# Two adjacent stages of a post-norm transformer kernel joined into one block, with the second stage's weight built inside the first

## The reference, cut to what matters

```
# sub-layer 5: 4-layer convolution stack on a 64-wide state (depth scan)
h = x @ Win.T + bin                                   # 512 -> 64
for i in range(4):
    y = silu(layernorm(h));  h = h + sconv(y) * sc    # a linear recurrence over the tokens
    y = silu(layernorm(h) @ W1.T + b1) @ W2.T + b2    # 64 -> 256 -> 64
    h = h + y
f5 = layernorm(h) @ Wout.T + bout                     # 64 -> 512
# sub-layer 6: dense layer with bias and two low-rank adapters (rank 64, scale 1/4)
f6 = x @ W_base.T + b_base + 0.25 * ((x @ A.T + x @ WL.T) @ B.T + (...) @ WR.T)
```

## Time and profile before

| quantity | value |
|---|---|
| median of three runs | 1443.9 us |
| time of the profiled execution | 1441.58 us |
| its span, first to last instruction | 1439.8 us |
| mean granted TensorE clock | 0.940 |
| busy: TensorE matmul / VectorE / ScalarE / GpSimd | 1294.9 / 745.1 / 431.1 / 151.4 us |
| start of the convolution block (first load issued) | 631.27 us |
| last instruction of the two-adapter block ends | 854.55 us |

### The profile page before, as it was taken

One profiled execution on the slowest core, in us unless ns is written; L12 is line 12 of the kernel. 1 busy time (PEld: TensorE's weight loads), 2 busy tenths in 40 slices (PEclk: granted clock), 3 DMA queues, 4 the chain that ended last, 5 costly groups with the idle time before them and its releaser, 6 DMA issues. The chain is left out here.

```text
span 1439.8 us, 14790 instructions
## 1 busy us (share of the span) xinstructions
PE 1294.9 (90%) x5410; PEld 853.0 (59%) x5410; DVE 745.1 (52%) x1297; ACT 431.1 (30%) x717; POOL 151.4 (11%) x208
## 2 busy tenths in 40 slices
PE   7999998799799999983887788989999998799998
PEld 4787665344578787772665343444454443488876
DVE  5222323484676645414576555877777632433264
ACT  2222211120311214200322112146666666221141
POOL 0000000000294000001111022001011114000000
PEclk9999999799899999975998799989999999899999
DMA  7110000730355530022000010000000000112000
GB/s 313 45 44 0 0 0 7 322 146 1 131 198 197 197 109 0 1 73 87 0 0 0 0 44 1 0 1 2 1 2 3 2 3 1 45 66 81 7 23 37
DMA packets 18072, 78.83 MB, mean 55 GB/s; under 512 B 2946, under 2 KB 3586, under 8 KB 15843
## 3 DMA queue, kind: packets, MB, share of 16 engines
q1 hardware_dynamic: 18018, 78.13, 14.8%
HBM read 75.76 MB, written 2.10 MB: 54 GB/s over the span
## 5 line engine op out<-in xcount | busy, mean ns | idle before, releaser
L373 PE MATMUL psum<-L_ffn_x,L_ffn_w_up 128*128 128x512 f32 x1152 | 264.3, 391 | 3.1 <-DVE L_ffn_hidden L502 3.1
L373 PEld LDWEIGHTS psum<-L_ffn_x,L_ffn_w_up 128*128 128x128 f32 x1152 | 217.0, 189 | 50.2 <-DVE L_ffn_hidden L502 5.0
L1830 DVE TENSOR_REDUCE mqa_top<-psum 128x1 f32<-128x512 f32 (+3 forms) x304 | 186.1, 657 | 57.4 <-PE psum L1656 37.7
L1749 ACT ACTIVATE mqa_prob<-psum 128x512 f32<-128x512 f32 x288 | 159.8, 601 | 85.7 <-PE psum L1674 84.5
L390 PE MATMUL psum<-L_ffn_wd,L_ffn_part_h 128*128 128x512 f32 x600 | 142.7, 399 | 7.0 <-DVE L_ffn_wd L298 7.0
L1674 PE MATMUL psum<-mqa_stack,mqa_keys 100*128 100x512 f32 x288 | 132.8, 476 | 4.8 <-DMA mqa_stack<-mqa_rows 3.5
L390 PEld LDWEIGHTS psum<-L_ffn_wd,L_ffn_part_h 128*128 128x128 f32 x600 | 114.9, 193 | 32.0 <-DVE L_ffn_part_h L289 7.8
L1645 PE MATMUL psum<-mqa_keys,mqa_stack 96*128 96x512 f32 (+1 forms) x256 | 107.3, 438 | 2.3 <-DVE mqa_top L1830 1.0
L373 PE MATMUL psum<-L_attn_x,L_attn_w_up 128*128 128x512 f32 x456 | 105.4, 393 | 3.9 <-DVE L_attn_hidden L502 3.9
L373 PEld LDWEIGHTS psum<-L_attn_x,L_attn_w_up 128*128 128x128 f32 x456 | 86.6, 190 | 22.5 <-issue 4.3
L1674 PEld LDWEIGHTS psum<-mqa_stack,mqa_keys 100*128 100x128 f32 x288 | 55.3, 196 | 72.1 <-ACT mqa_prob L1749 62.6
(11 more groups left out here) (247 smaller groups left out, 1716.3 us busy)
## 6 DMA issues: line engine op xcount, KB each, us to landing
L_ffn_stage<-in_L_w SPq DMA_DIRECT2D x25, 768.0 KB, 6.3
L_ffn_z_int<-in_L_z SPq DMA_DIRECT2D x14, 768.0 KB, 4.3
L_ffn_s_all<-in_L_s SPq DMA_DIRECT2D x14, 768.0 KB, 6.1
lora_wo<-in_L_wo SPq DMA_DIRECT2D x8, 1024.0 KB, 8.6
L_attn_stage<-in_L_w SPq DMA_DIRECT2D x10, 512.0 KB, 3.6
L_attn_w_down<-in_L_down SPq DMA_DIRECT2D x1, 2560.0 KB, 24.3
x_feat<-in_x_feat SPq DMA_DIRECT2D x2, 1024.0 KB, 7.2
x_tok<-in_x_tok SPq DMA_DIRECT2D x1, 2048.0 KB, 18.8
```

The costliest lines, as they stand in the source:

```text
L373: ins = nc.tensor.matmul(bank[half][:, :], w_up[:, slot, w_part, at:at + P], x[:, x_part, k, half * HALF:(half + 1) * HALF], start=k == 0 ...
L1749: nc.scalar.activation(prob[:, n % PROBS, :], score_bank[n % 3], ACT.Exp, scale=SCALE)\
L1830: nc.vector.tensor_reduce(top[:, i % 2, lo // HALF, heads[0]:heads[-1] + 1], max_bank[n % 3][:, 0:len(heads) * width] .rearrange("p (h k) ...
```

## The change: what it does, and the diff

The two blocks become one. `two_loras` is gone, and `conv_stack` receives its weights object, which now also owns `w_eff`, the sums and their semaphores.

1. SyncE waits for `loaded` (three loads) before it issues the ten loads of `load_ahead`.
2. GpSimd adds the adapter halves and scales one sum, before its first `root`; it no longer copies `W1` and the column constants.
3. The loops over the four layers are unrolled; layers read `w1_all[:, i]` and `cols[:, i]` directly.
4. Each layer i makes column block i of `W_eff` on TensorE: one matmul from the sums and one with the identity that adds the base weight; ScalarE copies the result out. The filler at a layer's end is 5 matmuls long, not 9. Eight filler matmuls stand ahead of the input projection and eight behind it.
5. The tail of sub-layer 5 and the product and tail of sub-layer 6 run as one pipeline: at step t come tile t of the first, and tile t-2 of the second. The second tail has banks 0 to 3 and semaphores of its own.
6. The bias is added to `x_tok` by GpSimd, after the tile's transposes and before the second tail's addition; VectorE's own bias addition (L97) is gone.

```diff
@@ sync
                 sp.dma_start(high[:, :], a["C_high"]).then_inc(loaded, 16)
+                sp.wait_ge(loaded, LOADS)
                 load_ahead(sp)
@@ gpsimd
-                def prepare(i, first):
-                    if not first:
-                        pool.wait_ge(ff_ready, 4 * i)
-                    nc.gpsimd.tensor_copy(w1[:, :], w1_all[:, i, :]).then_inc(w1_ready, 1)
-                    if not first:
-                        pool.wait_ge(hidden_ready, 4 * i)
-                    nc.gpsimd.tensor_copy(col[:, :], cols[:, i, :]).then_inc(col_ready, 1)
-                    root(2 * i)
-                    root(2 * i + 1)
-                prepare(0, True)
-                with pool.Fori(1, C_DEPTH) as i:
-                    prepare(i, False)
+                pool.wait_ge(two.loaded, 32)
+                nc.gpsimd.tensor_tensor(two.low_sum[:, :], two.low[:, 0, :], two.low[:, 1, :], ALU.add)\
+                    .then_inc(two.summed, 1)
+                nc.gpsimd.tensor_tensor(two.high_sum[:, :], two.high[:, 0, :], two.high[:, 1, :], ALU.add)\
+                    .then_inc(two.summed, 1)
+                pool.wait_ge(two.summed, 2)
+                nc.gpsimd.tensor_scalar(two.high_sum[:, :], two.high_sum[:, :], two.SCALING, None, ALU.mult)\
+                    .then_inc(two.summed, 1)
+                for n in range(2 * C_DEPTH):
+                    root(n)
                 root(2 * C_DEPTH)
+                pool.wait_ge(two.base_loaded, 32)
+                for t in range(NT):
+                    pool.wait_ge(tail.transposed, tail.base + t + 1)
+                    nc.gpsimd.tensor_tensor(c.x_tok[:, t, :], c.x_tok[:, t, :], two.bias[:, :], ALU.add)\
+                        .then_inc(two.biased, 1)
@@ tensor
+                keep_busy(8)
                 pe.wait_ge(in_loaded, 16)
...
-                    keep_busy(9)
+                    pe.wait_ge(two.summed, 3)
+                    pe.wait_ge(two.base_loaded, 32)
+                    nc.tensor.matmul(ff_bank[3][:, :], two.low_sum[:, i * P:(i + 1) * P], two.high_sum[:, :],
+                                     start=True, stop=False)
+                    nc.tensor.matmul(ff_bank[3][:, :], c.ident[:, :], two.base[:, i, :], start=False, stop=True)\
+                        .then_inc(two.made, 1)
+                    keep_busy(5)
+                keep_busy(8)
                 pe.wait_ge(const, 7)
-                with pe.Fori(0, C_DEPTH) as i:
+                for i in range(C_DEPTH):
                     layer(i)
...
+                pe.wait_ge(two.eff_ready, KC)
+                for t in range(NT + 3):
+                    if t < NT:
+                        if t >= 2:
+                            pe.wait_ge(tail.out_taken, tail.base + t - 1)
+                        nc.tensor.matmul(tail.out_bank[t % 2][:, :], normed2[:, t * P:(t + 1) * P], w_out[:, :],
+                                         start=True, stop=True).then_inc(tail.out_ready, 1)
+                    if 1 <= t <= NT:
+                        tail.pe(pe, t - 1)
+                    if 2 <= t < NT + 2:
+                        pe.wait_ge(tail.feat_ready, tail.base + t - 1)
+                        product_tiles(c, pe, tail_two, two.w_eff, t - 2)
+                    if t >= 3:
+                        tail_two.pe(pe, t - 3)
@@ scalar
+                    act.wait_ge(two.made, i + 1)
+                    nc.scalar.copy(two.w_eff[:, i, :], ff_bank[3][:, :]).then_inc(two.eff_ready, 1)
...
+                for t in range(NT + 3):
+                    if t < NT:
+                        tail.act_std(act, t)
+                    if 1 <= t <= NT:
+                        tail.act_copy(act, t - 1)
+                    if 2 <= t < NT + 2:
+                        tail_two.act_std(act, t - 2)
+                    if t >= 3:
+                        tail_two.act_copy(act, t - 3)
@@ vector
-                for t in range(NT):
-                    tail.dve(dve, t)
+                for t in range(NT + 2):
+                    if t < NT:
+                        tail.dve(dve, t)
+                    if t >= 2:
+                        dve.wait_ge(two.biased, t - 1)
+                        tail_two.dve(dve, t - 2)
```

More of the change, by code:

```diff
@@ L70, with __init__ @@
     NAMES = ("out_ready", "out_taken", "ln_step", "var_ready", "std_ready", "normed", "transposed", "feat_ready")
-    def __init__(self, chip, out_bank, tr_bank, last=False):
+    def __init__(self, chip, out_bank, tr_bank, last=False, sems=None):
         self.c, self.out_bank, self.tr_bank, self.last = chip, out_bank, tr_bank, last
         (self.out_ready, self.out_taken, self.ln_step, self.var_ready, self.std_ready, self.normed,
-         self.transposed, self.feat_ready) = chip.tail_sems
-        self.base = NT * chip.tails
-        chip.tails += 1
+         self.transposed, self.feat_ready) = chip.tail_sems if sems is None else sems
+        if sems is None:
+            self.base, self.steps = NT * chip.tails, chip.ln_steps
+            chip.tails += 1
+        else:
+            self.base, self.steps = 0, [0]
     def dve(self, dve, t, bias=None):
@@ L1164, in _ @@
                 ins.then_inc(h_in, 1)
-                def keep_busy(times):
-                    for _ in range(times):
-                        nc.tensor.matmul(ff_bank[0][:, 0:256], c.ident[:, :], rot.wave[:, 0, 0:256],
-                                         start=True, stop=True)
                 def transposes(n):
@@ L1195, in layer @@
                     transposes(2 * i + 1)
-                    pe.wait_ge(w1_ready, i + 1)
                     for half in range(2):
                         pe.wait_ge(n2_ready, 2 * i + half + 1)
+                        if i and half == 1:
+                            pe.wait_ge(two.eff_ready, i)
                         for f in range(FT):
-                            nc.tensor.matmul(ff_bank[2 * half + f][:, :], w1[:, f * P:(f + 1) * P],
+                            nc.tensor.matmul(ff_bank[2 * half + f][:, :], w1_all[:, i, f * P:(f + 1) * P],
                                              normed2[:, half * HALF:(half + 1) * HALF],
@@ L1236, in affine @@
                                              ACT.Identity, scale=weight, bias=bias).then_inc(n2_ready, 1)
-                with act.Fori(0, C_DEPTH) as i:
-                    act.wait_ge(col_ready, i + 1)
+                for i in range(C_DEPTH):
                     for half in range(2):
@@ L1305, in _ @@
                 PRE, STEPS = state_of["count"], 30
-                with dve.Fori(0, C_DEPTH) as i:
+                for i in range(C_DEPTH):
                     state_of["count"], state_of["base"] = PRE, STEPS * i
```

47 lines of the change are left out of this document (23 added, 24 removed).

## The result

The changed kernel takes 1424.99 us (median of 4 runs, 1422.25 to 1426.36); the kernel before, run beside it, 1443.57 (4 runs, 1441.13 to 1444.46). The ratio is 0.9876, 95% interval 0.9858 to 0.9893: faster by 18.6 us. The forecast was 1419.5 us, with a range of 1412 to 1429. The profiled executions took 1441.58 and 1424.28 us, 17.3 apart, where the sum of the prediction said 23.2.

A forecast was written before the change was run, and what follows sets the result against it. Bound by no engine in the layers, by VectorE then TensorE in turn behind them, by `conv_high` at the start. 22.2 + 0.8 + 1.2 - 1.0 = 23.2 us gave 1418.4, 1420.7 against the median; forecast 1419.5, range 1412 to 1429.

The forecast's parts named there:

- the sum of the prediction: All terms together against the profiled execution: 23.2 us gained, 1441.6 to 1418.4 us.
- Joined tails: Tails of sub-layers 5 and 6 in one loop: VectorE sets a 5.30 us period, 22.2 us gained.
- Bias on GpSimd: Joined loop: the 1.27 us addition per tile is hidden; 1 us charged for disturbing VectorE, bounds 0 and 10.
- rival 1: Joined loop: GpSimd and VectorE block each other in every tile, 10 us less gain, 1429.5 us; chance 0.09.
- SyncE's wait: Start of the block: holding back ten loads brings `conv_high` 4.0 us earlier, bounds 0 and 5.
- rival 2: Start: the ten loads are what delays `conv_high`, so `loaded` comes early; 11 us gained there, 1410 us; chance 0.07.
- The first root: GpSimd's first root at the start: 6.9 us after `loaded`, not 3.3; start's net gain 1.2 us, bounds -4 and 4.
- The halves: Start: adapter halves `two_low` and `two_high`, issued only after `loaded`, land 3.5 us after it.
- The scaling: GpSimd's scaling of an adapter sum before the first root: 0.8 us taken, from 0.4 to 1.3.
- Filler ahead of the projection: Start, TensorE: at most 7.4 us of filler at half clock, projection ends near 653, before the load; nothing gained or lost.
- Layers: Four unrolled convolution layers: 0.2 us saved in each, 0.8 us gain, bounds 0 and 2; making the adapter weight there costs nothing.
- Two of its signs: Signs of being right: attention's first matmul 23 us earlier; `loaded` 26 to 28 us after `conv_high` is issued.

The follow-up runs named there:

- Experiment 8: Changed kernel with the two tails one after the other, adapter weight still made in the layers, bias still on GpSimd: 1431.38 us, ratio 0.9913.
- experiment 1: Changed kernel with GpSimd's adapter additions and scaling moved from ahead of the first root to behind the second: 1419.28 us, ratio 0.9847.
- experiment 4: Changed kernel without SyncE's wait for `loaded`, its ten loads issued at once again: 1426.68 us, ratio 0.9899.
- experiment 3: Changed kernel with the 97-partition load `conv_high` issued as two, 96 partitions and 1: 1405.73 us, ratio 0.9753.
- Experiment 2: Changed kernel with a one-column dummy Silu on ScalarE ahead of its wait for the loads, so its table loads early: 1423.53 us, ratio 0.9874.
- the repeat: The changed kernel measured once more, with no edit: 1423.03 us, ratio 0.9864.
- experiments 9 and 10: Changed kernel with split load, later sums, early table; filler behind folding 7 to 4 matmuls, or behind first transposes 4 to 7: 1404.07 and 1404.90 us.
- experiment 5: The kernel before with only the 97-partition load issued as 96 and 1: 1428.19 us, ratio 0.9903.

## Why the prediction was right, and where it was not

*Joined tails, 22.2 forecast, 22.04 measured: right*, by its own steps. Period 5.30 us, clock at the upper level, the first product's four matmuls (eight records) 4.82 us for 4.3 (partly at the lower level), the end 52.06 us behind the first out matmul, where the sum had 51.9. (Its last addition, 827.6 + 2.75 + 1.7, makes 832.05 and not 832.3, and the copy's 1.51 and 0.58 us make more than 1.7; both slips are small.) Experiment 8 adds what the prediction didn't part: 13.0 of it needs no overlap.

*Bias on GpSimd, 1.0 charged of bounds 0 to 10: right*, and rival 1 false. The two pass each other, by as little as 0.04 us; only two of VectorE's steps were clearly longer. That the lock was real and the price small is shown by experiment 1's 1.48 us for 0.42.

*SyncE's wait, 4.0 us forecast, 4.8 measured, 5.0 by experiment 4: right in size.* By the load's own issue it was 6.1 us, above the bound of 5, so the ten loads had cost it more than "a few us"; the later issue took 1.3 back. The load's one engine was read rightly too, from the share of 0.06; rival 2 needed "loaded" within 12 us and is false. But the prediction used this finding only to bound the change. What it was worth, experiment 3 shows: 19 us.

*The first root is the step that failed.* The start was to gain 1.2 us and lost 2.05 to the first `y`. Three terms were mis-sized or missing:

- The halves: 3.5 us from "loaded" to their landing were taken from an issue of 0.5 us and 2.5 us for 256 KB. Measured 5.6: the two landed 3.9 and 4.5 us after their issues.
- The scaling: taken as 0.8 between two rows, measured 1.49, above the dearer bound of 1.3. Here 64x512 times a constant takes GpSimd longer than the addition of two such tensors (1.25). The root came 9.61 and not 6.9 us after "loaded".
- The table load, 1.28 us, was in no term. Experiment 2 shows it on the path. That ScalarE meets this load only behind its wait for the transposes was not read from the code.

Against that, two roots run back to back once the first can (2.02 us for both), since both variances were waiting.

*Filler ahead of the projection, nothing forecast: true of the sum, wrong in its reason.* The projection was to run at half clock and end near 653. It ran at the upper level and ended at 644.8, behind filler of 6.32 us; that bought nothing only because the load came at 658.96.

*Layers, 0.8 us gain forecast, 0.44 lost, 0.25 gained in the repeat: no gain shown.* The period where the clock holds is 26.42 us for 26.86, a gain of 0.44 each, twice what was forecast. (The prediction's 3.86 us for the two new matmuls and five of filler is 4.0 by its own prices, which changes nothing.) But the filler behind the folding is slow where the clock falls, and VectorE waits for what is queued behind it. Two layers of the changed kernel, filler and the row addition that waits, each:

```profile
734.72 5.41 PE L1116 MATMUL psum<-wave,ident 128*128 128x256 f32 x14
...
746.91 0.42 DVE L1305 TENSOR_TENSOR conv_h<-conv_h,psum 128x256 f32<-128x256 f32 x1 [7.23 <-PE psum L1164]
...
761.64 3.24 PE L1116 MATMUL psum<-wave,ident 128*128 128x256 f32 x14
...
773.33 0.42 DVE L1305 TENSOR_TENSOR conv_h<-conv_h,psum 128x256 f32<-128x256 f32 x1 [5.92 <-PE psum L1164]
```

Filler of 5.41 us, idle of 7.23 us; filler of 3.24, idle of 5.92. The granted clock is 0.59 over the first and 1.00 over the second. These seven matmuls (fourteen records) took 3.24 to 5.87 us over all kernels that have them, slow in different layers. What sets in which layer the clock falls stays open; experiments 9 and 10 moved it and did not explain it.

*After the block, nothing forecast, 1.04 us lost* to the first `mqa_k_full`, and 0.35 between the last copy and attention's first matmul. The first was 6.08 to 6.69 us in every kernel with the joined loop, and 5.46 in experiment 8, which has all of the change but that loop. So it belongs to the joined loop. The two stretches, of the kernel before and of the changed one:

```profile
855.02:860.54 5.52, 5.51 (x9) 2.44 (x10) 1.79 (x4) 0.00 (x0) 5.14 (x9) 0.68 0.44 147
```

```profile
835.89:842.45 6.56, 6.56 (x9) 2.87 (x10) 1.79 (x4) 0.00 (x1) 6.09 (x10) 0.57 0.52 166
```

TensorE is busy all through both, at a clock of 0.68 and 0.57. In the kernel before the clock is at the lower level from 851.7 to 858.5 us, 3.5 us of it in attention's matmuls; in the changed kernel from 834.7 to 841.5, 5.6 us of it. So the 1.04 us are the clock's, which fell later against attention's first matmul, 1.2 us ahead of it for 3.3. In the kernel before it fell in TensorE's pause ahead of the last transposes (849.7 to 852.8 us), in the changed one just behind them (they end at 834.4). What sets the moment isn't shown. The 0.35 us don't belong to the loop: that gap was 0.46 to 0.48 or 0.82 to 0.83 us in kernels with it, and 0.82 in experiment 8.

*The whole.* Of the 5.8 us between the sum (23.2) and the spans (17.4) the start has 3.25, the layers 1.24, attention's beginning 1.04 + 0.35, the 580 us behind it 0.7 and the time ahead of the block 0.07; the joined stage with the bias gave 0.84 more than the sum had. The direction and the main mechanism stand; the start's terms were mis-sized. The forecast of 1419.5 lay 1.2 us below the 1420.7 that the sum gives, and no term stands for that. Two of its signs were missed: attention's first matmul came 19.1 us earlier and not 23, and "loaded" 25.0 us after the load's issue and not 26 to 28.

## What to carry to other kernels

When the share of the DMA engines is one sixteenth during the wait that ends last, look at that load's partition count before anything else is tuned: here splitting 97 into 96 and 1 was worth as much as the whole restructuring. Work moved onto an idle engine is only free if it is put behind the small step for which the others wait; price what its inputs need to land too, from the moment they are issued. When two blocks are joined, part the gain into what is no longer waited for and what overlaps, since the first can often be had alone.

## What the runs showed that was not expected

- A load of 97 partitions and 596 kB is in 25 us after its issue and moves 26 GB/s; as 96 and 1 the same bytes are in within 7 us (633.22 to 639.92). The Trainium skill ("DMA: Bandwidth & Descriptors", section "Why a DMA increments its semaphore by 16 and not by 1") gives the rule by which a load's partition count sets on how many engines it runs, 16 for 96 partitions; experiments 3 and 5 agree with it in both kernels.
- With the ten loads right behind the load of 97 partitions, the issue of `two_high` kept SyncE for 7.65 us (experiment 4) and 7.41 us (the kernel before). With the ten just as close but that load split (experiment 5) it took 0.57 us. So it was not their number that held SyncE.
- GpSimd's scaling of 64x512 by a constant: 1.49 us, its addition of two such tensors: 1.25.
- With eight filler matmuls ahead of it the projection took 7.25 us for 13.92; seven filler matmuls in a layer took up to 5.87 us for 3.24 and then stood in the way of what they are to speed up.
